# Level-one high band of the second batch on GpSimd, and two of its synthesis tiles earlier on TensorE

## The chip, the cores and the metric

The kernel runs on one core of a Trainium2 chip. The metric is the device time of one execution in microseconds (us). A core has TensorE (PE in the profile), VectorE (DVE), ScalarE (ACT), GpSimd (POOL) and SyncE (SP, which here only issues DMAs). Each engine works through its own list of instructions in order; engines wait for each other by semaphores.

## The reference

The input `x` is 2 x 1024 x 128 (batch, sequence, channel). Two layers follow. The first is a two-level wavelet with attention in the middle:

```
x = x + attn(layernorm(x))
attn:  low = x
       for 2 levels:                      # depthwise convolution, 4 taps a channel
           l = dwconv(low, h_filter)[:, ::2]
           h = dwconv(low, g_filter)[:, ::2];  highs.append(h);  low = l
       low = linear_attention(low)        # 16 heads; q = k = elu(low)+1, v = low
       for h of level 2, then of level 1:
           low = dwconv(repeat(low, 2), h_synth) + dwconv(repeat(h, 2), g_synth)
       return layer_norm(x + low) * gamma + beta
x = x + moe(layernorm(x))
```

The second is a mixture of 16 experts: every expert takes its best 256 of the 2048 tokens, applies a gated two-matrix network of 512 hidden units, weighs the result by the score, and adds it to the tokens' rows; a shared network of 256 hidden units is added for all tokens. All of it is in 32-bit floats.

The change concerns `h` of the first level for the second batch: 512 positions of 128 channels, four taps each, from the normalised input, and its use in the last synthesis.

## The kernel before

**Layout.** In the wavelet stage channels are on the 128 partitions and positions in the columns. `xp[:, r, b, :]` holds the normalised input of batch `b` with even (r = 0) and odd (r = 1) positions apart, so that each of the four taps of a stride-two convolution is one operation over 512 columns: `PHASE[k]` gives for tap k which half, and at which offset. ScalarE writes the four halves of `xp` one after the other, each with an increment of `s_xp`; the fourth is batch 1, odd.

**Bands.** `l1p`, `h1p` are the low and high band of level one, `l2f` and `h2p` of level two. VectorE makes `l1p` of both batches (L805, L807), `l2f` (L816, L817), q (L837, L839), `h2p` (L816, L817 again), and `h1p` of batch 1 (`high1`, L827, L828). The high band of batch 0 is made by PE (L1127) and copied by ScalarE (`s_h1a`). Most VectorE operations of this stage depend on the one ahead of them and are joined by `link`, which waits for a semaphore of the engine's own.

**Attention.** PE turns `l2f` and then q (L1182, L1187) so that tokens are on the partitions, ScalarE copies them out (L614 is the exponential that q needs, L616 and L618 the copies), PE makes the key-value products (L1195) and, after VectorE has masked them (L849, L850), numerator and denominator (L1203); VectorE divides (L857 to L861), PE turns the result back (L1214), VectorE and ScalarE copy it (L867, L621).

**Synthesis.** The output of the last level is in four groups of 512 tokens (`bank[0]` to `bank[3]`, groups 0 and 1 are batch 0), each of four tiles of 128. A tile gets the normalised input (`add_xn`, L1148), the high band's products (`synth2_high`, 3 for an even tile, 2 for an odd one, all at L1155) and the low band's (`synth2_low`, L1155 too); a product is two instructions on PE. The group's sum of squares (ScalarE, L636) goes to GpSimd (`sum_scale`, L451, L452), whose scale VectorE uses in `block_out` (L903, L906), followed by the statistics of the next norm. A group's `turn_x1` (L1229) and `router` (L1258) follow on PE.

**GpSimd** makes constants (masks, identities, L461 to L486), adds `beta` to four tiles of the input after `s_r1v` (L491), makes the scales, then the products of the shared network (L508, L518), and at the end issues the gathers and scatters of the experts (L531, L542).

**Order.** All lists are written out by hand; there is no scheduler. PE's wait on the high band of batch 1 was ahead of group 2's products, after the low products of groups 0 and 1.

Of the kernel before, what the change touches and what calls it, by code (L numbers as in the profile page):

```python
# [11 lines left out]
ALU = mybir.AluOpType  # L12
# [15 lines left out]
def wavelet_attention_moe(nc, x, packed, weights, shared, down_b, out):  # L28
# [8 lines left out]
    N1, N2 = SEQ // 2, SEQ // 4  # L37
# [12 lines left out]
    with ctx:  # L50
# [3 lines left out]
        def sb(name, shape, dt=F32):  # L54
            return ctx.enter_context(nc.sbuf_tensor(name, shape, dt))

        def sem(name):
            return ctx.enter_context(nc.semaphore(name))
# [23 lines left out]
        taps = consts[:, 0:16]  # L82
# [12 lines left out]
        x1T = sb("x1T", [P, 2, 512])  # L95
# [13 lines left out]
        def carve(n, base=None):  # L109
            if base is not None:  # L110
                at[0] = base
            a = area[:, at[0]:at[0] + n]
            at[0] += n
            return a

        xn_tok = carve(2048, 0).rearrange("p (i c) -> p i c", i=NT)
        xp = carve(4 * 514).rearrange("p (r b n) -> p r b n", r=2, b=NB)
        l1p = carve(2 * 516).rearrange("p (b n) -> p b n", b=NB)
        h1p = carve(2 * 514).rearrange("p (b n) -> p b n", b=NB)
# [39 lines left out]
        sgate = sb("sgate", [P, 2, 512])  # L159
# [26 lines left out]
        sh_up = sb("sh_up", [P, 2, 512])  # L186
        sh_down = sb("sh_down", [P, 512])
        diag_c = sh_hid[:, :, :, :].rearrange("p s t n -> p (s t n)")[:, 0:10 * P].rearrange("p (k c) -> p k c", k=10)
        squares = sh_down[:, :].rearrange("p (t c) -> p t c", t=4)
        itab = sb("itab", [P, HI])  # L190
        rows = sb("rows", [P, CH, E], U32)
# [20 lines left out]
        s_xna = sem("s_xna")  # L212
        s_h1 = sem("s_h1")
        s_h1a = sem("s_h1a")
        s_h1v = sem("s_h1v")
        s_h2 = sem("s_h2")
        s_vT = sem("s_vT")
        s_kT = sem("s_kT")
# [18 lines left out]
        s_xp = sem("s_xp")  # L237
# [65 lines left out]
        PHASE = ((1, 0), (0, 1), (1, 1), (0, 2))  # L303
# [97 lines left out]
        def _(pool):  # L401
# [17 lines left out]
            for band, n in ((h1p, N1), (r1p, N1), (h2p, N2), (ap_, N2)):  # L419
                pool.memset(band[:, :, 0:1], 0.0)  # L420
                last = pool.memset(band[:, :, n + 1:n + 2], 0.0)
# [26 lines left out]
            def sum_scale(n):  # L448
# [7 lines left out]
            pool.iota(first_rows[:, :], pattern=[[0, 1]], base=0, channel_multiplier=1,  # L456
                      allow_small_or_imprecise_dtypes=True)

            pool.wait_ge(s_pick, len(SIZES))
            for n in SIZES:  # L460
                pool.memset(part[n][:, :, :], 1.0)  # L461
# [10 lines left out]
            def keep_block(t, first, pattern, n):  # L472

                return pool.affine_select(out=t, in_=t, compare_op=ALU.is_ge, fill=0.0, base=first, pattern=pattern,
                                          channel_multiplier=n)

            for n in SIZES:
                keep_block(part[n][:, :, :], 0, [[-8 * n, 2], [-n, 8]], 1)
                last = keep_block(seat[n][:, :, :], 0, [[-8 * n, 2], [0, n]], 1)
            link(last)  # L480
            for n in SIZES:
                keep_block(part[n][:, :, :], n - 1, [[8 * n, 2], [n, 8]], -1)
                last = keep_block(seat[n][:, :, :], 8 * n - 1, [[8 * n, 2], [0, n]], -1)
            link(last)
            for n in SIZES:
                last = pool.tensor_tensor(by_x[n][:, :], part[n][:, 0, :], part[n][:, 1, :], ALU.add)  # L486
# [3 lines left out]
            for i in range(8, 12):  # L490
                last = pool.tensor_tensor(x_tok[:, i, :], x_tok[:, i, :], beta_bc, ALU.add)  # L491
# [19 lines left out]
            for n in range(LAST):  # L511
                for t in range(SHT):
# [4 lines left out]
                    for k in range(0, 512, 64):  # L517
                        last = pool.tensor_tensor(sh_hid[:, n % 2, t, k:k + 64], sh_up[:, t, k:k + 64],  # L518
                                                  sgate[:, t, k:k + 64], ALU.mult)
# [222 lines left out]
        def _(dve):  # L742
            step = [0]

            def link(ins):

                step[0] += 1
                ins.then_inc(s_dve, 1)
                dve.wait_ge(s_dve, step[0])
# [49 lines left out]
            for b in range(NB):  # L799
                dve.wait_ge(s_xp, 2 * b + 2)  # L800
                dst = l1p[:, b, 1:N1 + 1]
                for k, (r, o) in enumerate(PHASE):
                    src = xp[:, r, b, o:o + N1]
# [16 lines left out]
                return dve.scalar_tensor_tensor(r1p[:, :, 1:N1 + 1:2], h2p[:, :, k:k + N2], tap_sum(1, k), part,  # L820
                                                ALU.mult, ALU.add)

            def high1(k):
                r, o = PHASE[k]
                dst, src = h1p[:, 1, 1:N1 + 1], xp[:, r, 1, o:o + N1]
                if k == 0:
                    return dve.tensor_scalar(dst, src, taps[:, 4:5], None, ALU.mult)  # L827
                return dve.scalar_tensor_tensor(dst, src, taps[:, 4 + k:5 + k], dst, ALU.mult, ALU.add)  # L828

            low2 = l2f[:, :].rearrange("p (b n) -> p b n", b=NB)  # L830
            high2 = h2p[:, :, 1:N2 + 1]
            for k in range(3):
# [43 lines left out]
                ins.then_inc(s_r1v, 1)  # L876

            finish_even(0)
            for k in range(3):
                link(high1(k))  # L880
            high1(3).then_inc(s_h1v, 1)
            finish_even(1)

            def add_beta(g):
# [54 lines left out]
            for k in range(3):  # L939
                dve.memset(ktab[:, k:k + 1], float(k + 1))  # L940
                last = dve.memset(cand[:, k:k + 1], float((k + 1) << ROUNDS[0]) - 0.5)
# [5 lines left out]
            for r, bit in enumerate(ROUNDS):  # L947
                unit = 1.0 if r < ROUNDS_HIGH else 2.0 ** -LOW
                for k in range(2):
                    last = dve.tensor_scalar(junk[:, k, :], keys, cand[:, k:k + 1], 0.0, ALU.is_ge, ALU.add,  # L950
                                             accum_out=cnt[:, k:k + 1])
# [15 lines left out]
                else:  # L967
                    link(dve.scalar_tensor_tensor(found, reached, unit, found_base, ALU.mult, ALU.add))
                    if keys is high:
# [3 lines left out]
                        for k in range(3):  # L973
                            last = dve.memset(cand[:, k:k + 1], float((k + 1) << ROUNDS[r + 1]) * 2.0 ** -LOW + 0.5 * 2.0 ** -LOW)
# [103 lines left out]
            for q in range(E * FT):  # L1078
# [11 lines left out]
                if 1 <= q < 1 + len(LATER):  # L1090
                    piece, quarter = LATER[q - 1]
                    last = piece(2, quarter * NT // 4, (quarter + 1) * NT // 4)
# [12 lines left out]
        def _(pe):  # L1105
# [38 lines left out]
            def add_xn(n):  # L1144
                pe.wait_ge(s_xp, 2 * (n // 2) + 2)
                for t in range(4):
                    b, par, m0, dst = place(n, t)
                    pe.matmul(dst, xp[:, par, b, m0 + 1:m0 + 1 + P], ident[:, :], start=(t == 0), stop=False,  # L1148
                              is_transpose=True, skip_group_check=True)
# [7 lines left out]
                return last  # L1157

            def synth2_high(n, those=range(4)):
                pe.wait_ge((s_h1a, s_h1v)[n // 2], 1)  # L1160
                pe.wait_ge(s_diag, 2)
                synth(n, those, h1p, 9)

# [17 lines left out]
            for k in range(4):  # L1181
                last = pe.transpose(bank[6][:, k * P:(k + 1) * P], l2f[:, k * P:(k + 1) * P], ident[:, :])  # L1182
# [3 lines left out]
            for k in range(4):  # L1186
                last = pe.transpose(bank[7][:, k * P:(k + 1) * P], qf[:, k * P:(k + 1) * P], ident[:, :])  # L1187
            last.then_inc(s_qvT, 1)
            add_xn(3)
            pe.wait_ge(s_vT, 1)  # L1190
            pe.wait_ge(s_kT, 1)
            for b in range(NB):
                for k in range(2):
                    i = 2 * b + k
                    last = pe.matmul(bank[6][:, b * 256:b * 256 + C + 1], kT[:, i * P:(i + 1) * P], vT[:, i, 0:C + 1],  # L1195
                                     start=(k == 0), stop=(k == 1))
# [3 lines left out]
            for b in range(NB):  # L1200
                for t in range(2):
                    o = (2 * b + t) * P
                    last = pe.matmul(bank[6 + b][:, t * (C + 16):(t + 1) * (C + 16)], qf[:, o:o + P], kvz[:, b, :],  # L1203
                                     start=True, stop=True)
# [6 lines left out]
            for b in range(NB):  # L1211
                pe.wait_ge(s_attn, b + 1)
                for t in range(2):
                    last = pe.transpose(bank[6 + b][:, t * P:(t + 1) * P], attn_tok[:, b, t, :], ident[:, :])  # L1214
                last.then_inc(s_attnT, 1)

            pe.wait_ge(s_diag, 4)
            pe.wait_ge(s_apv, 1)
# [10 lines left out]
                    last = pe.transpose(bank[6 + n % 2][:, t * P:(t + 1) * P], x1[:, 4 * n + t, :], ident[:, :])  # L1229
                last.then_inc(s_x1Tp, 1)  # L1230

            synth2_high(2)
            synth2_low(2)
            turn_x1(0)
            synth2_high(3)
# [34 lines left out]
            last = router(LAST)  # L1270
# [3 lines left out]
            for r in range(2):  # L1274
                last = pe.transpose(bank[5][:, r * P:(r + 1) * P], logits[:, r * P:(r + 1) * P], ident[:, :])
# [40 lines left out]
            for r in range(len(ROUNDS)):  # L1316
                count(r + 1)

                n, part = divmod(r, PERIOD)
# [9 lines left out]
            for k in range(2):  # L1329
                pe.wait_ge(s_mask, k + 1)  # L1330
                for r in range(2):
                    last = pe.matmul(bank[6 + k][:, r * P:(r + 1) * P], junk[:, k, r:256:2], ident_b[:, :],
                                     start=True, stop=True)
# [13 lines left out]
            for k in range(2):  # L1347
# [4 lines left out]
                last = pe.matmul(rank[k][:, P:2 * P], until[:, :], mask_T[:, k, 0:P], start=False, stop=True,  # L1352
                                 skip_group_check=True)
# [140 lines left out]
```

## Time and profile before

| | us |
|---|---|
| median of 3 runs | 206.1 (206.09 to 206.11) |
| span of the profiled execution | 204.6 |
| around the span, by the median | 1.5 |

The profiled execution has no time of its own beside its span; the runs differ by 0.02 us, so it is taken at their median. The page gives for each engine its busy time and share of the span; a busy share is an average over stages that have different limits. In the timeline a row is a start, a length (of several instructions of the same kind, from the first start to the last end), an engine, a line, and in brackets the idle time ahead of it with what ended it. In the chain of waits a row is a start, the length that the piece adds to the chain, and the piece.

The stages of the span: loading and first norm to about 13 us; wavelet, attention and synthesis to about 54; search for the best tokens, tables and shared network to about 96; experts to the end, where the scatters into the output come last.

### The profile page before, as it was taken

What the parts mean: (1) busy time and instruction counts of PE and PEld (TensorE: products, weight loads), DVE (VectorE), ACT (ScalarE), POOL (GpSimd) and SP (SyncE); (2) the same over time, 40 slices, a digit from 0 to 9 for tenths busy, and PEclk for the clock granted to TensorE, in tenths of its full rate; (3) what the DMA queues carried; (4) which work ended last, traced back from release to release, by engine and by line L of the source; (5) the groups of instructions that cost most, each with busy time, mean ns of one, the idle gap of its engine ahead of it and who ended that gap; (6) DMA issues with size and microseconds to landing.
All of it is one profiled execution on the core that took longest, in us unless ns stands there. A gap on an engine that the chain in (4) does not pass through costs nothing.

```text
span 204.6 us, 3620 instructions
## 1 busy us (share of the span) xinstructions
PE 181.2 (89%) x1196; PEld 156.4 (76%) x1196; DVE 125.5 (61%) x430; ACT 90.3 (44%) x239; POOL 127.5 (62%) x195
## 2 busy tenths in 40 slices
PE   6979898999979999998999999999999999957800
PEld 6947688999936677857899999999999889945700
DVE  4888999999878787785667644454445344422300
ACT  0687512448697768110344344444444345422210
POOL 7494005556117475927777888878878777866660
PEclk9999999999999999999999999999999999995875
DMA  5599999800030271104313323333233333332221
GB/s 149 182 411 419 420 419 419 363 12 3 0 117 0 99 225 51 49 23 138 91 44 42 43 42 45 54 40 42 43 47 53 40 40 29 40 40 21 20 24 13
DMA packets 11649, 22.26 MB, mean 109 GB/s; under 512 B 1504, under 2 KB 8800, under 8 KB 11504
## 3 DMA queue, kind: packets, MB, share of 16 engines
q1 hardware_dynamic: 5968, 17.52, 22.7%
q0 software_dynamic: 5664, 4.53, 16.1%
q8 instruction: 9, 0.15, 0.3%
q14 instruction: 8, 0.07, 0.1%
HBM read 17.72 MB, written 4.33 MB: 108 GB/s over the span
## 4 chain that ended last, share of the span: by engine, by line
PE 41%; DMA 15%; POOL 14%; issue 11%; DVE 10%; ACT 4%; POOLq 1%; SPq 1%; DVEq 0%; ACTq 0%
DMA out_dram<-area,rows 13%; POOL out_dram L542 9%; PE bank L1155 7%; PE bank L1434 4%; PE bank L1110 4%; PE bank L1435 4%; POOL hT L531 4%; PE bank L1296 4%; PE bank L1415 3%; PE bank L1308 3%; DMA x_tok<-in_x_dram 2%; PE bank L1258 2%; DVE junk L950 1%; DVE area L807 1%; DVE hT L817 1%
## 5 line engine op out<-in xcount | busy, mean ns | idle before, releaser
L542 POOL DMA_INDIRECT out_dram<-area,rows x32 | 50.7, 1584 | 16.8 <-DMA out_dram<-area,rows 8.7
L1086 DVE SCALAR_TENSOR_TENSOR area<-bank,consts,sgate 128x256 f32<-128x256 f32 x64 | 30.9, 483 | 42.4 <-ACT sgate L734 42.1
L734 ACT ACTIVATE sgate<-bank,consts 128x256 f32<-128x256 f32 x64 | 30.3, 473 | 53.3 <-PE bank L1435 53.1
L1434 PE MATMUL bank<-area,wT 128*128 128x256 f32 x128 | 40.3, 397 | 4.8 <-issue 4.1
L1415 PEld LDWEIGHTS bank<-wT,area 128*128 128x128 f32 x256 | 38.1, 191 | 4.1 <-DVE area L1086 1.0
L531 POOL DMA_INDIRECT hT<-h_rows,rows x32 | 31.9, 995 | 12.7 <-issue 9.1
L1435 PE MATMUL bank<-area,wT 128*128 128x256 f32 x128 | 39.3, 390 | 0.0
L1415 PE MATMUL bank<-wT,area 128*128 128x128 f32 x256 | 38.6, 275 | 0.6 <-DVE area L1086 0.6
L1435 PEld LDWEIGHTS bank<-area,wT 128*128 128x128 f32 x128 | 25.2, 197 | 3.7
L1434 PEld LDWEIGHTS bank<-area,wT 128*128 128x128 f32 x128 | 20.5, 198 | 6.2 <-issue 5.7
L518 POOL TENSOR_TENSOR sh_hid<-sh_up,sgate 128x64 f32<-128x64 f32 x48 | 13.7, 322 | 14.6 <-ACT sh_up L686 12.1
L1110 PE MATMUL bank<-ident 128*128 128x128 f32 x132 | 19.2, 304 | 1.6 <-POOL ident L411 1.6
L1110 PEld LDWEIGHTS bank<-ident 128*128 128x128 f32 x132 | 17.8, 215 | 2.1 <-POOL ident L411 1.6
L1155 PE MATMUL bank<-sh_hid,area 128*128 128x128 f32 x160 | 18.6, 276 | 0.0
L1155 PEld LDWEIGHTS bank<-sh_hid,area 128*128 128x128 f32 x160 | 18.2, 192 | 0.3 <-ACT area L609 0.3
L1296 PE MATMUL bank<-hT,sh_wT 128*128 128x512 f32 x32 | 17.3, 629 | 0.6 <-ACT hT L650 0.6
L563 ACT ACTIVATE area<-area,hT 128x128 f32<-128x128 f32 x32 | 11.0, 392 | 10.3 <-DVE area L1074 10.3
L950 DVE TENSOR_SCALAR_CACHE_REDUCE junk<-area,search 128x256 bf16<-128x256 f32 (+1 forms) x30 | 13.2, 477 | 1.3 <-ACT area L664 0.8
L491 POOL TENSOR_TENSOR x_tok<-x_tok,consts 128x128 f32<-128x128 f32 x4 | 3.2, 816 | 15.1 <-DVE area L873 15.1
L1074 DVE TENSOR_TENSOR area<-bank,x_tok 128x256 f32<-128x256 f32 x16 | 6.7, 419 | 9.0 <-DMA out_dram<-area,rows 8.2
L1308 PEld LDWEIGHTS bank<-sh_wT,sh_hid 128*128 128x128 f32 x64 | 8.4, 191 | 4.4 <-issue 3.3
L446 POOL TENSOR_TENSOR rstd<-var_eps,half_pow 128x4 f32<-128x4 f32 (+1 forms) x6 | 7.4, 1232 | 6.6 <-DVE var_eps L762 6.6
(195 smaller groups left out, 259.1 us busy)
## 6 DMA issues: line engine op xcount, KB each, us to landing
wT<-in_weights_dram SPq DMA_DIRECT2D x16, 768.0 KB, 16.2
h_rows<-hrow SPq DMA_DIRECT2D x2, 576.0 KB, 3.7
x_tok<-in_x_dram SPq DMA_DIRECT2D x4, 256.0 KB, 3.9
x_tok<-in_down_b_dram SPq DMA_DIRECT2D x1, 1024.0 KB, 6.2
out_dram<-x SPq DMA_DIRECT2D x4, 256.0 KB, 2.1
hT<-h_rows,rows POOLq DMA_INDIRECT x32, 2.6
out_dram<-area,rows POOLq DMA_INDIRECT x32
sh_wT<-in_shared_dram SPq DMA_DIRECT2D x1, 384.0 KB, 2.9
```

The source lines that it names most:

```text
L531: pool.indirect_dma_start(out=gath[:, e % GBUF, c, :], out_offset=None, in_=h_rows[:, :], in_offset=bass.IndirectOffsetOnAxis(ap=rows[:, c ...
L542: pool.indirect_dma_start(out=out_rows, in_=eo[:, e % 2, c, :], in_offset=None, out_offset=bass.IndirectOffsetOnAxis(ap=rows[:, c, e:e + 1 ...
L734: act.activation(sgate_e[:, q % SGB, :], up_bank(q)[:, CAP:2 * CAP], ACT.Silu, bias=biasT[:, 1, j, e:e + 1]).then_inc(s_sil, 1)
L950: last = dve.tensor_scalar(junk[:, k, :], keys, cand[:, k:k + 1], 0.0, ALU.is_ge, ALU.add, accum_out=cnt[:, k:k + 1])
L1086: dve.scalar_tensor_tensor(hidden[:, e % 2, j, :], up_bank(q)[:, 0:CAP], biasT[:, 0, j, e:e + 1], sgate_e[:, q % SGB, :], ALU.add, ALU.mul ...
L1110: pe.matmul(spare[:, 0:P], ident[:, :], ident[:, :], start=True, stop=True)
L1155: last = pe.matmul(dst, band[:, b, m0 + o:m0 + o + P], diag_c[:, d0 - 4 + k, :], start=False, stop=(d0 == 4 and o == 2), skip_group_check= ...
L1296: pe.matmul(bank[2 * kind + t][:, :], sh_wT[:, 2 * kind + t, :], rhs, start=True, stop=True).then_inc((s_shg, s_shu)[kind], 1)
L1308: last = pe.matmul(bank[6 if n == LAST else 4][:, t * P:(t + 1) * P], sh_hid[:, n % 2, k, t * P:(t + 1) * P], sh_wT[:, 4 + k, :], start=(k ...
L1415: last = pe.matmul(bank[3 + e % 2][:, c * P:(c + 1) * P], hidden[:, e % 2, j, c * P:(c + 1) * P], wT[:, e, 2, j, :], start=(j == 0 and c = ...
L1434: pe.matmul(up_bank(q)[:, 0:CAP], wT[:, e, 0, j, :], xselT[:, e % 2, :], start=True, stop=True)
L1435: pe.matmul(up_bank(q)[:, CAP:2 * CAP], wT[:, e, 1, j, :], xselT[:, e % 2, :], start=True, stop=True).then_inc(s_gu, 1)
```

## The change

VectorE's four operations of `high1` go. GpSimd makes the same band in seven: four products of `xp` and a tap, the first into `h1p` and three into buffers that are free at that time (`x1T`, `sgate`), and three additions, each waiting for the one ahead of it. They stand behind the norm scales and in front of the constants. On PE, the second and the first tile of group 2's high-band products move up: one behind `add_xn(3)`, in front of the key-value products, one behind the turn of the attention's result; two tiles stay.

```diff
@@ tensors
+        tap_products = (x1T[:, 0, :], x1T[:, 1, :], sgate[:, 0, :])
@@ gpsimd
             pool.iota(first_rows[:, :], ...)
+            def high1(k):
+
+                r, o = PHASE[k]
+                dst, src = h1p[:, 1, 1:N1 + 1], xp[:, r, 1, o:o + N1]
+                into = tap_products[k - 1] if k else dst
+                return pool.tensor_scalar(into, src, taps[:, 4 + k:5 + k], 0.0, ALU.mult, ALU.add)
+
+            pool.wait_ge(s_xp, 4)
+            for k in range(4):
+                last = high1(k)
+            link(last)
+            for k in range(3):
+                last = pool.tensor_tensor(h1p[:, 1, 1:N1 + 1], h1p[:, 1, 1:N1 + 1], tap_products[k], ALU.add)
+                if k < 2:
+                    link(last)
+            last.then_inc(s_h1p, 1)
             pool.wait_ge(s_pick, len(SIZES))
@@ vector
-            def high1(k):
-                r, o = PHASE[k]
-                dst, src = h1p[:, 1, 1:N1 + 1], xp[:, r, 1, o:o + N1]
-                if k == 0:
-                    return dve.tensor_scalar(dst, src, taps[:, 4:5], None, ALU.mult)
-                return dve.scalar_tensor_tensor(dst, src, taps[:, 4 + k:5 + k], dst, ALU.mult, ALU.add)
...
             finish_even(0)
-            for k in range(3):
-                link(high1(k))
-            high1(3).then_inc(s_h1v, 1)
             finish_even(1)
@@ tensor
-                pe.wait_ge((s_h1a, s_h1v)[n // 2], 1)
+                pe.wait_ge((s_h1a, s_h1p)[n // 2], 1)
...
             add_xn(3)
+            synth2_high(2, (1,))
             pe.wait_ge(s_vT, 1)
             pe.wait_ge(s_kT, 1)
...
                 last.then_inc(s_attnT, 1)
+            synth2_high(2, (0,))
...
-            synth2_high(2)
+            synth2_high(2, (2, 3))
             synth2_low(2)
```

On GpSimd, before, the constants (`part`, `seat` and on) follow the norm scales and the first row numbers at once:

```order
L446 TENSOR_TENSOR rstd<-var_eps,half_pow 128x8 x2
L456 IOTA first_rows 128x1
L461 MEMSET part 128x16
L463 COPY seat<-own 128x4 x2
L461 MEMSET part 128x16
L463 COPY seat<-pick 128x8 x2
```

and after the change seven operations of 512 columns stand there (`area` holds `xp` and `h1p`, `consts` the taps), all constants behind them:

```order
L447 TENSOR_TENSOR rstd<-var_eps,half_pow 128x8 x2
L457 IOTA first_rows 128x1
L465 TENSOR_SCALAR area<-area,consts 128x512
L465 TENSOR_SCALAR x1T<-area,consts 128x512 x2
L465 TENSOR_SCALAR sgate<-area,consts 128x512
L472 TENSOR_TENSOR area<-area,x1T 128x512 x2
L472 TENSOR_TENSOR area<-area,sgate 128x512
L478 MEMSET part 128x16
```

What moved: nothing ahead of the seven; everything behind them on GpSimd waits until they are done.

On PE, before, from the turn of `l2f` (`hT` holds `l2f` and q) to the end of group 2's products; `sh_hid` holds the synthesis matrices, `hrow` the turned keys:

```order
L1182 MATMUL bank<-ident,hT 128x128 x4
L1148 MATMUL bank<-ident,area 128x128 x4
L1187 MATMUL bank<-ident,hT 128x128 x4
L1148 MATMUL bank<-ident,area 128x128 x4
L1195 MATMUL bank<-hrow 128x129 x4
L1155 MATMUL bank<-sh_hid,area 128x128 x5
L1203 MATMUL bank<-kvz,hT 128x144 x4
L1172 MATMUL bank<-area,diag 128x256 x4
L1214 MATMUL bank<-ident,attn_tok 128x128 x4
L1172 MATMUL bank<-area,diag 128x256 x4
L1155 MATMUL bank<-sh_hid,area 128x128 x40
```

and after the change:

```order
L1189 MATMUL bank<-ident,hT 128x128 x4
L1155 MATMUL bank<-ident,area 128x128 x4
L1194 MATMUL bank<-ident,hT 128x128 x4
L1155 MATMUL bank<-ident,area 128x128 x4
L1162 MATMUL bank<-sh_hid,area 128x128 x2
L1203 MATMUL bank<-hrow 128x129 x4
L1162 MATMUL bank<-sh_hid,area 128x128 x5
L1211 MATMUL bank<-kvz,hT 128x144 x4
L1179 MATMUL bank<-area,diag 128x256 x4
L1222 MATMUL bank<-ident,attn_tok 128x128 x4
L1162 MATMUL bank<-sh_hid,area 128x128 x3
L1179 MATMUL bank<-area,diag 128x256 x4
```

What moved: of the 40 products behind the last of these rows 35 are left; two now wait for the band ahead of the key-value products, three ahead of the first synthesis's last part.

## Rows read from the trace of the kernel before

**Rows 1.** The page, part 1: busy us of each engine, share, instructions.

```profile
PE 181.2 (89%) x1196; PEld 156.4 (76%) x1196; DVE 125.5 (61%) x430; ACT 90.3 (44%) x239; POOL 127.5 (62%) x195
```

**Rows 2.** Chain of waits in order of time, 15 to 55 us: start, us, piece.

```profile
18.38 0.76 DVE area L807
...
23.54 0.67 PE bank L1187 x4
...
24.96 1.13 PE bank L1195 x8
26.09 1.12 PE bank L1155 x10
27.21 1.11 PE bank L1203 x8
...
33.31 8.93 PE bank L1155 x80
```

**Rows 3.** Timeline of VectorE, 18 to 62 us: start, us, instructions, idle before.

```profile
19.69 2.33 DVE L817 SCALAR_TENSOR_TENSOR hT<-area,consts,hT 128x512 f32<-128x512 f32 x3
...
22.80 0.69 DVE L839 SCALAR_TENSOR_TENSOR hT<-hT 128x512 f32<-128x512 f32 x1 [0.32 <-ACT hT L614]
...
38.53 1.12 DVE L903 SCALAR_TENSOR_TENSOR x<-bank,sum_var,consts 128x128 f32<-128x128 f32 x4
```

**Rows 4.** Timeline of GpSimd, 10 to 62 us.

```profile
11.40 0.11 POOL L461 MEMSET part<- 128x16 f32 x1
...
16.90 0.88 POOL L486 TENSOR_TENSOR by_x<-part 128x8 f32<-128x8 f32 x2
32.91 3.15 POOL L491 TENSOR_TENSOR x_tok<-x_tok,consts 128x128 f32<-128x128 f32 x4 [15.14 <-DVE area L873]
...
37.10 1.20 POOL L452 TENSOR_TENSOR sum_var<-sum_var,half_pow 128x4 f32<-128x4 f32 x1
```

**Rows 5.** Timeline of PE, 18 to 70 us.

```profile
18.19 3.62 PE L1155 MATMUL bank<-sh_hid,area 128*128 128x128 f32 x30
...
24.96 1.13 PE L1195 MATMUL bank<-hrow 128*128 128x129 f32 x8 [0.33 <-ACT hrow L618]
...
31.35 1.97 PE L1172 MATMUL bank<-area,diag 128*128 128x256 f32 x8 [0.77 <-DVE area L867]
```

**Rows 6.** GpSimd's groups by shape: count, busy us, mean ns of one.

```profile
L518 POOL TENSOR_TENSOR sh_hid<-sh_up,sgate 128x64 f32<-128x64 f32 x48 | 13.7, 322 | 14.6 <-ACT sh_up L686 12.1 <-issue 2.5
...
L508 POOL TENSOR_TENSOR x<-sh_down,x 128x128 f32<-128x128 f32 x8 | 3.4, 457 | 0.0
...
L451 POOL TENSOR_SCALAR sum_var<-sum_var 128x4 f32<-128x4 f32 x3 | 0.6, 198 | 2.0 <-ACT sh_down L636 2.0
...
L431 POOL TENSOR_SCALAR neg_half<-same 128x128 bf16<-128x128 f32 x1 | 0.3, 308 | 0.0
```

**Rows 7.** Timeline in narrow windows, single instructions of VectorE and GpSimd together.

```profile
33.20 0.82 DVE L828 SCALAR_TENSOR_TENSOR area<-area,consts 128x512 f32<-128x512 f32 x1
33.44 0.90 POOL L491 TENSOR_TENSOR x_tok<-x_tok,consts 128x128 f32<-128x128 f32 x1
34.06 0.83 DVE L828 SCALAR_TENSOR_TENSOR area<-area,consts 128x512 f32<-128x512 f32 x1
...
76.13 0.45 POOL L508 TENSOR_TENSOR x<-sh_down,x 128x128 f32<-128x128 f32 x1
76.20 0.40 DVE L964 SCALAR_TENSOR_TENSOR search<-search 128x3 f32<-128x3 f32 x1
```

**Rows 8.** Windows: busy us of each engine, PE's granted clock (1.00 is full).

```profile
9.60:13.00 3.40, 1.89 (x15) 1.36 (x14) 2.73 (x12) 2.99 (x7) 3.14 (x12) 1.00 1.02 411
...
181.00:184.00 3.00, 0.98 (x7) 0.69 (x6) 0.39 (x1) 0.00 (x0) 1.67 (x2) 0.95 0.42 37
184.00:187.00 3.00, 1.42 (x4) 1.18 (x5) 0.76 (x2) 0.69 (x2) 1.80 (x2) 0.50 0.06 7
```

More of the change, by code:

```diff
@@ L214, in wavelet_attention_moe @@
         s_h1a = sem("s_h1a")
-        s_h1v = sem("s_h1v")
+        s_h1p = sem("s_h1p")
         s_h2 = sem("s_h2")
```

## The prediction

> **What bounds the kernel now.** I read the page's busy shares first, to see whether one engine fills the span: TensorE (PE) is busy for 181.2 us, VectorE (DVE) for 125.5, GpSimd (POOL) for 127.5 of 204.6 [rows 1]. No engine but PE is full, and GpSimd looks like an engine with room. That is an average, so I went on to the chain of waits in order of time, for the stretch that the change touches. Between 16 and 33 us the chain goes from one engine to the next: the filter taps on VectorE, an exponential on ScalarE, one more VectorE operation, transposes on PE, a copy on ScalarE, the key-value products on PE at 24.96. From 33.31 on it is PE alone, 8.93 us of synthesis products without a gap [rows 2]. In that second stretch VectorE is as full: it starts the block output of group 0 at 38.53 [rows 3]; its scale, which GpSimd makes, is ready at 37.10 + 1.20 = 38.30 [rows 4]. GpSimd's gap is before that: from the end of its constants at 17.8 to the beta adds at 32.9 it waits [rows 4].
>
> So two places count. In 18 to 27 us VectorE sets the pace: its operations stand end to end, three linked taps taking 2.33 us (0.78 each, of which 0.75 is the operation) [rows 3]. In 33 to 54 us PE and VectorE run beside each other.
>
> **The change part by part.**
>
> *Four VectorE operations leave* (one scaling at 33 us and three multiply-adds, 3.1 us at the taps' 0.78). They lie beside PE's products, and VectorE is only 0.23 us later than GpSimd's scale when it begins the block output (38.53 against 38.30) [rows 3, 4]. When they go, that scale is what is late next. I count -0.2 us.
>
> *Five high-band products leave PE's full stretch.* 80 instructions take 8.93 us, two to a product, so a product is 0.22 us and five are 1.1 [rows 2]. The stretch behind them is shared with VectorE's block output, which I have just priced: PE gets to group 2 sooner and waits there. I count nothing, and -1.1 if VectorE were not the limit. Two of the products now stand ahead of the key-value products, where PE waits 0.33 us for ScalarE's copy; 0.45 us there is 0.1 too long [rows 5]. VectorE's own work up to its first use of those products covers that tenth. Three stand where PE waits 0.77 us for VectorE: 0.67 us fits [rows 5].
>
> *Seven GpSimd operations come in at about 18.3 us*, when the fourth phase copy is there, beside VectorE's last tap of level one (18.38 [rows 2]), and with them the question. How long is one? Additions of 64 and of 128 columns take 0.322 and 0.457 us: 2.1 ns for each further column, so 512 columns take 1.26. A scaling goes from 0.198 (4 columns) to 0.308 (128), 0.9 ns a column: 0.65 at 512; if all of the 0.308 went with the columns, 1.2 [rows 6]. Four scalings and three additions with their links would be some 6.5 us alone: done at 24.7, just when PE comes for them. Alone is what they are not.
>
> *What the two engines do to each other.* The beta adds of before run beside the VectorE operations that now go, and their rows show it [rows 7]. The add that starts at 33.44 takes 0.90, twice its 0.457: it ends at 34.34, 0.32 us after the multiply-add beside it ended (34.02). The next multiply-add starts at 34.06 and ends at 34.89, 0.55 after the add: it takes 0.83, where the taps of 18 to 27 us take 0.75. So they go in turns, and a VectorE operation that follows a linked one bears 0.24 us of GpSimd in front of it (0.03 until it starts, 0.20 of its own start) before it is late: 0.32 - 0.24 = 0.08, as measured. A three-element operation at 76.20 took 0.40 and ended with the 128-column add beside it (76.60 against 76.58) [rows 7]. Of the add's 0.457 us a hold of 0.32 shows, 0.14 less; for a scaling of 128 columns the same count gives 0.308 - 0.14 = 0.17.
>
> The rows are all for 128 columns or fewer; at 512 I must choose. If a turn costs VectorE 0.08 whatever the size, seven cost 0.6. If a turn lasts as long as GpSimd's columns, an addition holds 0.32 + 384 x 2.1 ns = 1.13 us and costs VectorE 0.89; a scaling holds 0.17 + 0.34 = 0.51 and costs 0.27. I take the second, because the multiply-add began its stream at the end of the add, not at some share of it. The Trainium skill bears on this choice (SBUF — State Buffer, "Who interferes with whom"): it has the shared port pair as an exclusive lock that is held for the whole instruction. The alternation in rows 7 agrees; by that rule the dear end holds, by an equal share of bandwidth the cheap one would.
>
> In turns, from 18.4 on: the four scalings go ahead of the last tap of level one, the first of level two and two more: 4 x 0.27 = 1.08. The additions, each linked to the one before, go ahead of the last tap, of the maximum and of the multiply-add that ends q: 3 x 0.89 = 2.67. Of the 3.75 us, 0.3 is covered: ahead of that last operation VectorE waited 0.32 for the exponential anyway, which by then is done [rows 3]. So q comes 3.4 us late, at 26.9; all that follows is on the chain: transposes, copy, key-value products, attention, first synthesis. The band itself is done at about 26.5, and PE asks for it at 28: the wait is not what costs, the port is. The bounds of this term are 0.6 - 0.3 = +0.3 and, with scalings at 1.2 us (0.55 more each, 2.2), +5.6.
>
> *GpSimd's constants* (6.4 us, in 11.4 to 17.8 before [rows 4]) are now behind the band, 26.5 to about 33. The beta adds behind them wait for an event that moves to 36: covered, with 3 us to spare.
>
> *PE's clock.* PE would stand from 21.8 [rows 5] to 24.0 and again until 26.9, with 1.3 us of transposes between: a quarter of five microseconds. In before, the granted clock stays at its upper level (2.4 GHz) with 1.89 us busy of 3.40 (9.6 to 13.0), and falls to the lower one (1.2 GHz) where PE has 0.98 busy of 3.00 (181 to 184); 184 to 187 is at 0.50 [rows 8]. Mine is emptier than the stretch that fell, so I expect a fall. At half clock the chain's PE pieces from 27 to 35 us (now 0.67, 1.13, 1.12 and 1.11 us, 4.0 [rows 2]) would cost at most 4 more; if the fall comes and goes within the wait, nothing. I take +1.0, nearer the lower end, because PE also has slack beside VectorE there.
>
> Sum: 3.4 - 0.2 + 1.0 = +4.2 us. The profiled execution has a span of 204.6 us; the runs are at 206.1 (206.09 to 206.11), so 1.5 us lie around the span, and I take that as unchanged: 210.3 us. Behind 54 us the kernel is one long chain (search, tables, experts, scatter), so I expect the delay to pass through whole.
>
> **The rivals.**
> 1. *Turns cost little.* VectorE loses 0.08 us a turn, GpSimd fits its columns beside it. Then +0.3 and the -0.2: 206.2, no change. For: the 0.08 measured. Against: the three-element operation that waited out the whole add [rows 7].
> 2. *Faster.* The band is made wholly beside VectorE, PE waits for nothing, and the shorter PE stretch is worth a little beyond the 0.2: 205.3 to 205.6. For: 6.5 us of GpSimd in a gap of 15, and the two products in PE's own gaps. Against: rows 7, each of them. It decides itself by the three taps behind 19.7 us: if they are still 0.75 each, this is the case.
> 3. *PE stalls on the band.* GpSimd, not VectorE, loses the turns: at the 0.90 us that 128 columns took beside VectorE, an addition of 512 is 3.6 and the seven operations take some 14 us, to 32.5. Two products wait for them ahead of the key-value products, in PE's order: 32.5 - 24.6 = 7.9 us late, less 0.2, 213.8. This is the queue's wait; it decides from the point where the band is later than q's transposes. Against: the 0.90 is mostly waiting, and a wait does not grow with columns.
> 4. *A middling turn*, half the stated hold at 512 columns or no fall of the clock: 207 to 209.
>
> **How the numbers follow.** My forecast (turns as long as the columns, with or without the whole of the clock's term, 209 to 211.8) has 0.66; rival 1 0.08; rival 2 0.05; rival 3 0.08; rival 4 0.13. About 0.4 us (0.2%) is what a measurement can tell from no change. Faster is rival 2: 0.05. Rival 1 and a little of 4 make "same": 0.09. Slower: 0.86. The range from 206.9 to 212.0 leaves out rivals 1, 2 and 3, 0.2 together.
>
> **What would show it.** Right: the last tap of level two and the two operations of q on VectorE at 1.2 to 1.7 us instead of 0.75 and less, each ending about half a microsecond after a GpSimd addition; the key-value products at about 28.5 instead of 24.96; no PE wait on GpSimd there; a granted clock of 0.5 some time between 23 and 32. Wrong: taps at 0.75 to 0.85 (then rivals 1 or 2), or PE waiting for GpSimd's last addition (rival 3). If q is 3.4 us late but the end is not, something behind 54 us has slack that I took as none.

## The result

The changed kernel takes 210.84 us (median of 4 runs, 209.8 to 212.33), the kernel before 206.11 (206.09 to 206.24, 4 runs). The ratio is 1.024, 95% interval 1.021 to 1.027: slower. The profiled execution is the run of 209.8 us, the shortest of the four, with a span of 208.0 (204.6 before). The four runs lie 2.5 us apart, where those of before lay within 0.2; what is known of that is told with the experiments.

Part 1 of the page after the change:

```profile
PE 180.8 (87%) x1196; PEld 156.5 (75%) x1196; DVE 126.5 (61%) x426; ACT 90.3 (43%) x239; POOL 136.8 (66%) x202
```

VectorE has four operations fewer and is busy for longer, 126.5 us against 125.5 [rows 1]: what it lost in operations came back in longer ones. GpSimd is busy for 9.3 us more; its seven operations take it from 16.38 to 24.88. The timeline of VectorE shows where its own time went:

```profile
16.32 0.49 DVE L822 TENSOR_SCALAR area<-area,consts 128x512 f32<-128x512 f32 x1 [0.61 <-ACT area L608]
16.84 3.26 DVE L824 SCALAR_TENSOR_TENSOR area<-area,consts 128x512 f32<-128x512 f32 x3
20.14 0.80 DVE L833 TENSOR_SCALAR hT<-area,consts 128x512 f32<-128x512 f32 x1
20.98 4.46 DVE L834 SCALAR_TENSOR_TENSOR hT<-area,consts,hT 128x512 f32<-128x512 f32 x3
25.46 0.46 DVE L847 TENSOR_SCALAR hT<-hT 128x512 f32<-128x512 f32 x1
26.21 0.69 DVE L849 SCALAR_TENSOR_TENSOR hT<-hT 128x512 f32<-128x512 f32 x1 [0.28 <-ACT hT L631]
...
42.23 1.13 DVE L910 SCALAR_TENSOR_TENSOR x<-bank,sum_var,consts 128x128 f32<-128x128 f32 x4 [2.08 <-POOL sum_var L453]
```

The three taps of level two (L834, L817 before) take 4.46 us instead of 2.33 [rows 3], the three of level one 3.26, also instead of 2.33. q ends at 26.90, 3.4 us later than at 23.49 [rows 3]. The last row answers to 38.53 [rows 3]: VectorE now waits 2.08 us for GpSimd's scale, which is what was to be late next. GpSimd's own timeline has the other half of the turns:

```profile
16.38 0.98 POOL L465 TENSOR_SCALAR area<-area,consts 128x512 f32<-128x512 f32 x1 [4.84 <-ACT area L608]
17.34 2.22 POOL L465 TENSOR_SCALAR x1T<-area,consts 128x512 f32<-128x512 f32 x2
19.54 1.12 POOL L465 TENSOR_SCALAR sgate<-area,consts 128x512 f32<-128x512 f32 x1
20.74 2.64 POOL L472 TENSOR_TENSOR area<-area,x1T 128x512 f32<-128x512 f32 x2
23.46 1.42 POOL L472 TENSOR_TENSOR area<-area,sgate 128x512 f32<-128x512 f32 x1
...
36.98 2.62 POOL L508 TENSOR_TENSOR x_tok<-x_tok,consts 128x128 f32<-128x128 f32 x4 [5.30 <-DVE area L883]
```

and single instructions of both in narrow windows, as in rows 7:

```profile
22.47 1.46 DVE L834 SCALAR_TENSOR_TENSOR hT<-area,consts,hT 128x512 f32<-128x512 f32 x1
23.46 1.42 POOL L472 TENSOR_TENSOR area<-area,sgate 128x512 f32<-128x512 f32 x1
23.97 1.47 DVE L834 SCALAR_TENSOR_TENSOR hT<-area,consts,hT 128x512 f32<-128x512 f32 x1
```

A tap ends at 23.93; the addition that waited beside it ends at 24.88, 0.95 later; the next tap ends at 25.44, 0.56 after the addition. That is the pattern of rows 7 (0.32 and 0.55) with an addition four times as wide. PE's timeline has the rest:

```profile
25.49 1.12 PE L1189 MATMUL bank<-ident,hT 128*128 128x128 f32 x4 [3.60 <-DVE hT L834]
...
27.25 1.06 PE L1194 MATMUL bank<-ident,hT 128*128 128x128 f32 x4
28.10 0.75 PE L1155 MATMUL bank<-ident,area 128*128 128x128 f32 x4
28.69 0.61 PE L1162 MATMUL bank<-sh_hid,area 128*128 128x128 f32 x4
29.14 1.07 PE L1203 MATMUL bank<-hrow 128*128 128x129 f32 x8
```

PE waits 3.60 us for level two, and the transposes behind the wait take 1.12 and 1.06 us where the last ones before took 0.67 [rows 2]. The windows say why (behind each stretch stand its length and PE's busy time; third from the end is the granted clock, 1.00 for 2.4 GHz):

```profile
21.80:25.00 3.20, 0.09 (x1) 0.00 (x0) 3.13 (x3) 0.00 (x0) 3.04 (x5) 1.00 1.02 414
25.00:28.40 3.40, 2.91 (x14) 2.92 (x15) 3.01 (x6) 1.27 (x3) 3.17 (x10) 0.50 1.01 413
28.40:31.00 2.60, 2.60 (x25) 2.60 (x24) 1.96 (x6) 2.00 (x6) 2.53 (x9) 1.00 1.02 418
```

After 3.2 us with 0.09 us busy on PE the clock is at 1.2 GHz (0.50) from 25.0 to 28.4. The key-value products start at 29.14 instead of 24.96 [rows 2]: 3.4 us from VectorE, some 0.8 from the clock. The two high-band products that were moved ahead of them (L1162 at 28.69) wait for nothing: the band is done at 24.88.

### The profile page after: what moved, and what is told of

It reads as the page before. It is cut to its first block, busy times and chain, and to the rows that moved or that the text cites. A ratio compares the mean times of both kernels' runs of the same rounds, so it can differ in the third digit from the quotient of the medians.

```text
span 208.0 us, 3625 instructions
## 1 busy us (share of the span) xinstructions
PE 180.8 (87%) x1196; PEld 156.5 (75%) x1196; DVE 126.5 (61%) x426; ACT 90.3 (43%) x239; POOL 136.8 (66%) x202
## 4 chain that ended last, share of the span: by engine, by line
PE 40%; DVE 14%; POOL 13%; issue 12%; DMA 10%; ACT 7%; POOLq 1%; SPq 1%; DVEq 0%; ACTq 0%
DMA out_dram<-area,rows 8%; POOL out_dram L559 8%; PE bank L1443 6%; PE bank L1444 5%; PE bank L1424 4%; PE bank L1117 4%; POOL hT L548 4%; PE bank L1305 4%; PE bank L1317 3%; DMA x_tok<-in_x_dram 2%; PE bank L1162 2%; DVE hT L834 2%; PE bank L1179 2%; DVE stats L774 2%; DVE area L824 2%
## 5 line engine op out<-in xcount | busy, mean ns | idle before, releaser
L1443 PE MATMUL bank<-area,wT 128*128 128x256 f32 x128 | 39.8, 393 | 4.7 <-issue 4.0
L1444 PE MATMUL bank<-area,wT 128*128 128x256 f32 x128 | 38.9, 386 | 0.0
L1444 PEld LDWEIGHTS bank<-area,wT 128*128 128x128 f32 x128 | 24.9, 195 | 3.5
L1117 PE MATMUL bank<-ident 128*128 128x128 f32 x132 | 18.4, 295 | 1.6 <-POOL ident L412 1.6
L1162 PE MATMUL bank<-sh_hid,area 128*128 128x128 f32 x160 | 18.9, 276 | 0.0
L1162 PEld LDWEIGHTS bank<-sh_hid,area 128*128 128x128 f32 x160 | 18.4, 192 | 0.3 <-ACT area L626 0.3
L1117 PEld LDWEIGHTS bank<-ident 128*128 128x128 f32 x132 | 17.0, 206 | 2.1 <-POOL ident L412 1.6
L695 ACT ACTIVATE below<-area,search 128x256 bf16<-128x256 f32 (+1 forms) x15 | 7.6, 508 | 4.8 <-DVE search L971 4.0
```

The lines of the kernel that those rows point to most:

```text
L1117: pe.matmul(spare[:, 0:P], ident[:, :], ident[:, :], start=True, stop=True)
L1162: last = pe.matmul(dst, band[:, b, m0 + o:m0 + o + P], diag_c[:, d0 - 4 + k, :], start=False, stop=(d0 == 4 and o == 2), skip_group_check= ...
L1443: pe.matmul(up_bank(q)[:, 0:CAP], wT[:, e, 0, j, :], xselT[:, e % 2, :], start=True, stop=True)
L1444: pe.matmul(up_bank(q)[:, CAP:2 * CAP], wT[:, e, 1, j, :], xselT[:, e % 2, :], start=True, stop=True).then_inc(s_gu, 1)
```

## The experiments

Theory: GpSimd's operations read through a port that VectorE needs, in turns, each for as long as its columns take; q is late by the sum, and PE's wait for it costs clock on top. Each time is compared with runs of the kernel before on the same chip, made together with it; they have medians of 206.05, 206.19 and 206.31 us, and single runs from 205.6 to 208.2.

**1. The tiles back in their old place.** Rival: the two products that wait for the band ahead of the key-value products.

```diff
             add_xn(3)
-            synth2_high(2, (1,))
...
-            synth2_high(2, (0,))
...
-            synth2_high(2, (2, 3))
+            synth2_high(2)
```

> The changed kernel with all four high-band tiles of group 2 back in their old place on TensorE; GpSimd's seven operations stay. Theory (turns at the port): VectorE's taps behind 16.8 us still take about 1.06 and 1.46 us, level two ends near 25.4, q near 26.9, and the time stays at 209.5 to 212.5 us, within 0.6 of the changed kernel. Rival (the queue): the two products that wait for the band ahead of the key-value products hold TensorE up; then the time falls to 206.5 or less.

210.44 us (209.77 to 210.88) against 206.05, ratio 1.021 (1.019 to 1.023). Level two ends at 25.14 and q at 26.60, 13.5 us behind the first tap of level one as in the changed kernel (13.38 to 26.90; before 13.29 to 23.49, 10.2). The products' place is not the cause of q's delay, nor of most of the time. The clock in this profile is low for longer, 24.3 to 31.0.

**2. Only one of the seven operations.** Three of the band's four taps are left out.

```diff
-            for k in range(4):
-                last = high1(k)
...
+            high1(0).then_inc(s_h1p, 1)
```

> The changed kernel with only the first of GpSimd's seven operations; three of the four taps of that band are left out of the result. Everything else stays: VectorE without its four operations, the new order on TensorE, the constants behind the band. Theory: one tap of VectorE takes 1.06 us, the others 0.75, q is 0.3 us late, no fall of the clock, 205.7 to 206.4 us. Rival (the new order on GpSimd or TensorE costs by itself): 207.5 us or more.

206.32 us (205.73 to 208.11, 10 runs) against 206.05, ratio 1.003 (1.001 to 1.006). The level-one taps in the timeline:

```profile
16.70 2.64 DVE L817 SCALAR_TENSOR_TENSOR area<-area,consts 128x512 f32<-128x512 f32 x3
```

One of three is 0.31 longer, the others are at 0.75. Seven runs lie at 205.7 to 206.4. In the profile, of a run of 205.93, q is 0.3 us late, as one turn has it, and from q to the block output it is 14.7 us instead of 15.0: the new order and VectorE's relief bring nearly 0.4 us back. By that, an estimate of what a band for nothing could win here is 0.4 us. Three runs at 207.9 to 208.1 were not expected; two of them have a lower mean granted clock (0.961 and 0.962, the others 0.965 to 0.970), the third has 0.973, and their cause is open.

**3. A turn by its size.** Into the kernel before:

```diff
+            pool.wait_ge(s_xp, 4)
+            for n in (64, 128, 256, 384, 512):
+                link(pool.tensor_tensor(x1T[:, 0, 0:n], xp[:, 0, 1, 1:1 + n], xp[:, 1, 1, 1:1 + n], ALU.add))
```

> The kernel before, with five additional additions on GpSimd from 16.3 us on, of 64, 128, 256, 384 and 512 columns, each waiting for the one ahead of it, into a buffer that nobody reads; VectorE makes the band as before. Theory: the VectorE operation behind each is late by about 0, 0.1, 0.3, 0.5 and 0.7 us; together 1.5, and 207.3 to 208.5 us. Rival (a turn costs the same whatever the size): 0.1 each, 206.5 us.

208.27 us (one run). Narrow windows of both engines, the VectorE row behind each addition of 128, 256, 384 and 512 columns:

```profile
16.76 0.83 DVE L810 SCALAR_TENSOR_TENSOR area<-area,consts 128x512 f32<-128x512 f32 x1
...
17.63 1.10 DVE L810 SCALAR_TENSOR_TENSOR area<-area,consts 128x512 f32<-128x512 f32 x1
...
18.77 1.11 DVE L819 TENSOR_SCALAR hT<-area,consts 128x512 f32<-128x512 f32 x1
19.67 1.33 POOL L461 TENSOR_TENSOR x1T<-area 128x512 f32<-128x512 f32 x1
19.91 1.64 DVE L820 SCALAR_TENSOR_TENSOR hT<-area,consts,hT 128x512 f32<-128x512 f32 x1
```

Against 0.75 (0.49 for the scaling at 18.77) that is 0.08, 0.35, 0.62 and 0.89: 0.27 for each further 128 columns, 2.1 ns a column, the slope of rows 6; 384 and 512 columns cost more than the 0.5 and 0.7 expected. The rival of one price for all sizes is out. 0.89 is what the prediction had for an addition; in the changed kernel it is 0.71.

**4. GpSimd as busy, but reading nothing.** Into the kernel before:

```diff
+            pool.wait_ge(s_xp, 4)
+            for _ in range(14):
+                link(pool.memset(x1T[:, 0, :], 0.0))
```

> The kernel before with 14 fills of 512 columns added on GpSimd from 16.3 us on, each waiting for the one ahead of it, into a buffer that nobody reads: GpSimd is as busy as with the band, until 24 us or later, and its constants come as late, but it reads nothing. Theory (the cost is GpSimd's reading beside VectorE): VectorE's taps stay at 0.75 to 0.80 us, q is at most 0.3 us late, 206.0 to 206.5 us. Rival (GpSimd's being busy, or its constants' coming late, is what costs): 208 us or more.

207.10 us (206.1 to 207.9, 10 runs) against 206.19, ratio 1.004 (1.001 to 1.006): more than expected, and less than the rival. The timeline of GpSimd in this kernel:

```profile
16.36 8.76 POOL L461 MEMSET x1T<- 128x512 f32 x14 [4.80 <-ACT area L594]
```

and that of VectorE beside it:

```profile
16.33 0.83 DVE L808 TENSOR_SCALAR area<-area,consts 128x512 f32<-128x512 f32 x1 [0.61 <-ACT area L594]
17.20 2.33 DVE L810 SCALAR_TENSOR_TENSOR area<-area,consts 128x512 f32<-128x512 f32 x3
19.56 0.68 DVE L819 TENSOR_SCALAR hT<-area,consts 128x512 f32<-128x512 f32 x1
20.27 2.33 DVE L820 SCALAR_TENSOR_TENSOR hT<-area,consts,hT 128x512 f32<-128x512 f32 x3
22.64 0.69 DVE L840 TENSOR_SCALAR hT<-hT 128x512 f32<-128x512 f32 x1
```

With GpSimd busy for as long (8.76 us), the multiply-adds, which read two tensors, are untouched (2.33 for three), so it is GpSimd's reading that costs them. The scalings, with one input, are longer (0.83, 0.68 and 0.69 instead of 0.53, 0.49 and 0.43): a fill holds them up though it reads nothing. This is as the Trainium skill has it (SBUF — State Buffer, "Who interferes with whom"): an operation with two SBUF inputs meets GpSimd's reads alone, one in a two-port mode any use of the pair. The untouched multiply-adds agree; that the scalings run in such a mode no run shows. q is 0.5 late; the rest of the 0.9 at the end was not traced.

**5. The constants back in front.** The band, from its wait to its event, stands behind the last of the constants:

```diff
-            pool.wait_ge(s_xp, 4)
-            for k in range(4):
-                last = high1(k)
...
             last.then_inc(s_masks, 1)
...
+            pool.wait_ge(s_xp, 4)
+            for k in range(4):
+                last = high1(k)
...
```

> The changed kernel with GpSimd's constants back in front of the band, which then starts near 18 us instead of 16.4. Theory: the same seven turns, four scalings at 0.31 and three additions at 0.71, but two VectorE operations later, so that the last two additions fall on q's two operations and 0.3 us are covered by the wait for the exponential; q 3.0 to 3.1 us late, 209.3 to 211.5 us. Rival (the constants' place makes the loss): 206.5 to 207.5 us.

211.46 us (211.12 to 211.67) against 206.19, ratio 1.025 (1.020 to 1.029). The turns are where expected, the last two on q's operations, which took 0.43 and 0.69 before:

```profile
23.71 1.20 DVE L847 TENSOR_SCALAR hT<-hT 128x512 f32<-128x512 f32 x1
24.95 1.46 DVE L849 SCALAR_TENSOR_TENSOR hT<-hT 128x512 f32<-128x512 f32 x1
```

q ends 13.40 us behind the first tap, 3.2 late. The constants' place is not the cause. The clock is at its lower level from 25.6 to 32.4 here, which the range's upper end allowed for.

**6. Fillers for the clock.** PE's wait for level two filled with products of the identity, once with the tiles as changed, once with the tiles of experiment 1:

```diff
             synth2_high(1, range(2))
+            stay_warm(14, bank[7])
             pe.wait_ge(s_l2, 1)
```

> The changed kernel with 14 filler products of the identity on TensorE (about 3.3 us) in its wait for the end of level two. Theory: the granted clock stays at 1.00 through 20 to 32 us, the key-value products start near 28.4 instead of 29.3, and the median is 208.7 to 209.3 us, with all runs within 0.6 us of each other. Rival (the clock's fall costs nothing, or the spread of the runs comes from elsewhere): 209.8 to 212.3 as in the changed kernel.

209.60 us (208.94 to 211.23, 6 runs) against 206.05, ratio 1.020 (1.017 to 1.023). In the profile, of the run of 208.94, the clock is at 1.00 from 5.4 to 186 us, and the key-value products start 1.5 us behind q (26.33) as in the kernel before (24.96, 23.49); in the changed kernel it was 2.2:

```profile
27.81 1.13 PE L1204 MATMUL bank<-hrow 128*128 128x129 f32 x8
```

So the fall is real and the fillers keep it away. But the median is above the 209.3 expected and the runs are 2.3 us apart still: that part of the expectation did not hold. The two longest, 210.5 and 211.2, have the same mean granted clock as the shortest, 0.966, so that their length is the clock's is not shown.

> The changed kernel with the 14 fillers and with all four tiles of group 2 in their old place. Theory: the clock's first fall is kept away by the fillers and its second, near 54 us, by TensorE's full stretch, so every run lies within 0.6 us of the others, at 209.0 to 209.8 us: 3.4 us for the turns, less at most 0.3. Rival (the spread of 2 us comes from the tail of the kernel): runs from 209 to 211.5 us as with the fillers alone.

209.67 us (209.37 to 209.93, 5 runs) against 206.31, ratio 1.017 (1.015 to 1.018): within 0.6 of each other, as expected. The clock is at 1.00 from 5.4 to 186 us in its profile too. With no fall of the clock left there, the turns by themselves are worth 209.67 - 206.31 = 3.4 us at the end of the kernel. The two kernels differ in the tiles' place alone, so the spread goes with that place, as far as six and five runs tell.

**7. The changed kernel again**, for the spread.

> The changed kernel once more, unaltered, for a second profile and more runs, since its four runs lay at 209.8, 210.0, 211.7 and 212.3 us and the kernel with one scaling showed 2 us more in 3 of 10 runs. Theory: the runs differ in how long the clock stays at its lower level between 23 and 33 us; a run of 211 us or more has two stretches of it there, or a lower mean clock than one of 209.9. Rival (a second cause behind 54 us): slow and fast runs with the same mean clock.

Six runs at 209.58 to 212.13, median 211.33. Their mean granted clock: 0.962 and 0.963 for 209.6 and 210.1, 0.953 and 0.954 for the four from 210.8 to 212.1; the first four runs have 0.962 and 0.964 at 209.8 and 210.0, 0.946 at 211.7 and 212.3. So in this kernel the long runs are those with the lower clock. The profiled run is the one of 212.13, and it has a second fall, outside the 23 to 33 us where the theory looked for it. Its windows (columns as above):

```profile
50.70:54.10 3.40, 3.06 (x28) 2.82 (x26) 3.26 (x15) 3.17 (x14) 2.01 (x4) 1.00 0.00 0
54.20:57.50 3.30, 3.30 (x18) 3.30 (x17) 3.13 (x16) 0.87 (x3) 1.58 (x3) 0.50 0.02 5
```

PE's timeline there:

```profile
52.78 1.06 PE L1267 MATMUL bank<-gate_cT,x1T 128*128 128x16 f32 x8 [0.34 <-ACT x1T L663]
53.70 2.91 PE L1117 MATMUL bank<-ident 128*128 128x128 f32 x14
56.40 1.06 PE L1238 MATMUL bank<-ident,x 128*128 128x128 f32 x4
```

The clock falls at 54.2, and 14 filler instructions take 2.91 us. From the block output (L910) to the turn of the scores (L1284) it is 17.0 us here and 15.8 in the first profile: 1.3 us. The products moved ahead have PE at the router (L1267) early, where it waits 0.34 us for ScalarE's copy, and one could take that wait for the reason. But the first profile has the same wait and as much busy time, and its clock stays up:

```profile
50.70:54.10 3.40, 3.05 (x27) 2.81 (x27) 3.26 (x17) 3.19 (x14) 2.63 (x5) 1.00 0.02 5
```

```profile
52.17 1.07 PE L1267 MATMUL bank<-gate_cT,x1T 128*128 128x16 f32 x8 [0.35 <-ACT x1T L663]
53.08 1.81 PE L1117 MATMUL bank<-ident 128*128 128x128 f32 x14
```

So that wait alone does not bring the fall, and why it comes in one run and not in the other is open.

**8. The band in pieces.** Constants in front, tiles in their old place, and

```diff
+            for c in range(0, N1, 128):
+                for k in range(4):
+                    r, o = PHASE[k]
+                    into = tap_products[k - 1][:, c:c + 128] if k else h1p[:, 1, 1 + c:129 + c]
+                    last = pool.tensor_scalar(into, xp[:, r, 1, o + c:o + c + 128], taps[:, 4 + k:5 + k], 0.0, ALU.mult, ALU.add)
+            link(last)
+            for k in range(3):
+                for c in range(0, N1, 128):
+                    into = h1p[:, 1, 1 + c:129 + c]
+                    last = pool.tensor_tensor(into, into, tap_products[k][:, c:c + 128], ALU.add)
...
```

> The changed kernel with the constants in front of the band, the band in 28 operations of 128 columns instead of seven of 512, and all tiles of group 2 in their old place. Theory: a piece gets one turn beside each VectorE operation and holds it 0.17 (scaling) or 0.32 us (addition), so the taps stay under 0.84 us and q is at most 0.6 us late; but the band is done only near 38 us, and GpSimd's beta adds and the scale of group 0 stand behind it: block output near 42 instead of 38.5, 209 to 211 us. Rival (a turn costs the same whatever the size): taps at 1.06 or more, q 3 us late or more, 213 us or more.

206.60 us (205.87 to 207.11, 8 runs) against 206.19, ratio 1.001 (0.999 to 1.004). VectorE's timeline in this kernel:

```profile
16.55 2.33 DVE L829 SCALAR_TENSOR_TENSOR area<-area,consts 128x512 f32<-128x512 f32 x3
18.92 0.49 DVE L838 TENSOR_SCALAR hT<-area,consts 128x512 f32<-128x512 f32 x1
19.45 2.33 DVE L839 SCALAR_TENSOR_TENSOR hT<-area,consts,hT 128x512 f32<-128x512 f32 x3
```

and two rows of GpSimd's, the first piece of the fourth scaling and the last additions:

```profile
19.63 0.81 POOL L501 TENSOR_SCALAR sgate<-area,consts 128x128 f32<-128x128 f32 x1
...
32.43 2.13 POOL L506 TENSOR_TENSOR area<-area,sgate 128x128 f32<-128x128 f32 x4
```

The taps are what they were without GpSimd, and q is on time (23.25, 10.2 us behind the first tap). The same arithmetic on the same engine makes q 3.2 us later in seven operations (experiment 5, constants in front too) than in 28. The time was lower than expected, since the band was done at 34.6 and not 38: where VectorE reads PSUM or waits, between 26 and 31 us, most pieces go through at 0.37 to 0.41, half of the 0.81 beside the taps. The block output starts 25.5 us behind the first tap instead of 25.2: VectorE waits 2.57 us for the scale, which stands behind the beta adds.

**9. An attempt at a faster one**: the pieces, the beta adds behind the first two scales, and two fillers fewer on PE; beside it the kernel before with the two fillers fewer alone.

```diff
-            WARM_T = (0, 0, 7, 0)
+            WARM_T = (0, 0, 5, 0)
```

> The band in pieces of 128 columns, constants first, all tiles of group 2 in their old place, and besides GpSimd's beta adds behind the scales of groups 0 and 1, and 5 instead of 7 filler products on TensorE ahead of the turn of group 3. Theory: taps at 0.75 us, q as in the kernel before; the block output starts 0.3 to 0.4 us earlier, since VectorE no longer makes the band and GpSimd's scale has nothing ahead of it; the chain behind it follows: 205.5 to 205.9 us. Rival (nothing to win there, TensorE is the limit): 206.0 to 206.4 us.

> The kernel before with 5 instead of 7 filler products, nothing else. Theory: VectorE, which makes the band, is the limit up to the scores, so TensorE waits instead: 206.0 to 206.2 us, no change. Rival (the fillers are the limit): 205.6 us.

206.41 us (205.76 to 207.99, 12 runs), ratio 1.002 (0.999 to 1.005), and 206.79 (205.76 to 208.61, 12 runs), ratio 1.003 (1.000 to 1.007), against 206.31. In the profile of the first the block output comes 24.9 us behind the first tap of level one instead of 25.2, as expected. At the end nothing of it can be told: its five lower runs (205.8 to 206.1) lie where the lower runs of the kernel before lie (from 205.8). Four and six of the twelve runs lie above 207.2; of the kernel before three in 63, of the pieces with seven fillers none in eight. Neither profile was of such a run. A second fall of the clock does not show in them: one of the ten has a mean granted clock of 0.962, the other nine 0.966 to 0.972, and the shorter runs beside them have 0.966 to 0.974, where the long runs of experiment 7 had 0.009 less. Their cause is open. Nothing here beats the kernel before.

## Why the prediction was right, and where its steps were not

The forecast was 210.3, the measurement 210.8, and the cause is the one it named: turns with GpSimd that last as long as its columns. That the number came so near is in part luck, as two sizes were off in opposite ways and a start was wrong. Step by step:

- *Who sets the pace, and what is late next*: right. VectorE waits for GpSimd's scale (2.08 us); the beta adds behind the constants wait 5.30 us for their event, so the constants were covered (experiment 5 has them in front and is no faster).
- *The start of the seven operations*: wrong. It was put at 18.3, as by the ScalarE copy that ends near 18.1; that copy is of batch 0's band. The fourth phase copy is done at 16.2 in the kernel before, 16.3 after the change, and GpSimd starts at 16.38. So all seven turns fell ahead of the end of level two, the exponential covered nothing, and the band was ready at 24.88, not 26.5. The sign that q's two operations would take 1.2 to 1.7 us failed for that reason: they take 0.46 and 0.69, and the turns are on the taps.
- *The price of a turn*: the rule was right (longer with the columns, experiment 3), two sizes were off. A scaling cost VectorE 0.31 (1.06 against 0.75) and not 0.27, an addition 0.71 (1.46 against 0.75) and not 0.89: 4 x 0.31 + 3 x 0.71 = 3.4. The forecast had 3.75 less 0.3 of cover, 3.4 as well: two misses that cancel, which is luck. Why the band's additions, which write over one of their inputs, hold 0.95 and that of experiment 3 1.12 was not tried.
- *PE's products ahead*: their wait cost nothing, as said. That the clock can fall once more behind them was missed: 1.3 us in the run of 212.1. That the products ahead are the reason is argued from the spread of the runs with and without them (2.3 and 0.6 us, experiment 6), not shown.
- *The clock*: the fall came in the stretch named. Its term was 1.0; from q to the block output the changed kernel takes 15.3 us in the first profile and 16.1 in the second, with the fillers 14.8: 0.6 and 1.4 that far. At the median the change costs 4.7 us, 1.3 more than the turns; the forecast had 1.0 - 0.2 for that.
- *The -0.2*: experiment 2 puts it, with the products ahead, at 0.4; with the tiles in their old place nothing of it reached the end (experiment 6: 3.3 at q, 3.4 at the end). PE then starts the second turn (L1237) 23.6 us behind q, as before (23.5); with the products ahead it was 22.5.
- *The delay passes whole*: right. q to the last instruction is 181.1 us in both first profiles, but in the later one the clock's loss and VectorE's relief are in that sum; the cleaner sign is experiment 6, with the tiles in their old place and no fall.

## What to carry to other kernels

An engine with idle time is not free if its reads hold up another engine, as GpSimd's did VectorE's here: before moving work to GpSimd, look for a place in the old trace where both run, and measure from the end of the one to the end of the other. If the work has to go there, cut it to pieces that fit between two operations of VectorE; 128 columns were free here, 512 were not. And the clock can differ from run to run of one kernel: look at its rows in more than one profile.

## What was not expected of the hardware

A fill on GpSimd, which reads nothing, lengthened VectorE's one-input scalings by 0.2 to 0.3 us and left its two-input multiply-adds alone. TensorE's clock fell at 54.2 us behind a stretch in which the profile has it busy for 3.06 of 3.40 us, with transposes, fillers and products of 16 columns; it did not fall in the first profile behind 3.05 of 3.40 in the same place, nor in the kernel before where PE was busy for 1.89 of 3.40 [rows 8]. So busy time in these rows does not tell a fall from none.
